# A transformer block on one core: routing weights and local values copied through DRAM instead of through TensorE

## The reference

```python
xn = layernorm(x)
# attention: 16 heads of 8 dimensions, causal; 4 heads see all earlier keys, 12 see the last 32
qkv = xn @ w_qkv + b_qkv
w = softmax(where(mask, -inf, q k^T * 8 ** -0.5))
s = (w v) @ w_out + b_out
# mixture of experts: E = 16 experts, 4 are used for a token
scores = sigmoid(xn @ gate_w.T)
cw = top-4 of the allowed groups, normalised, * 2.5, 0 elsewhere     # [tokens, 16]
act = silu(xn Wg[e]^T) * (xn Wu[e]^T)                                # 64 wide for each expert
y = sum over e of cw[:, e] * act[e] @ Wd[e]^T  + shared expert
out = x + s * silu(xn + y)
```

## Time and profile before

| | |
|---|---|
| median of 3 runs | 541.29 us (541.35, 535.84, 541.29) |
| the profiled execution's own time | 535.39 us |
| its span, first to last instruction | 533.6 us |
| TensorE's mean granted clock | 0.988 |
| busy: PE, DVE, ACT, POOL | 479.1, 347.8, 329.1, 269.0 us |
| one BODY section | about 122 us |

### The profile page before, as it was taken

The page is one execution under the profiler, slowest core; times in us unless marked ns, Lnnn a source line. Parts: engine busy times, 40 slices in busy tenths (PEclk is TensorE's granted clock), DMA queues, the critical chain, the costliest instruction groups (busy, mean ns, idle before and its releaser), DMA issues.

```text
span 533.6 us, 10570 instructions
## 1 busy us (share of the span) xinstructions
PE 479.1 (90%) x3832; PEld 286.6 (54%) x3832; DVE 347.8 (65%) x755; ACT 329.1 (62%) x654; POOL 269.0 (50%) x239
## 2 busy tenths in 40 slices
PE   1859978899999989899999988999999998989995
PEld 0647554555446755555446765545546765544442
DVE  7876439775977638776787546776788532676414
ACT  3536753767956554666957556475976566366972
POOL 3407942265737852254655872145664963016623
PEclk9979999999999999999999999999999999899998
DMA  9275374000450575000350387000170178000001
GB/s 214 79 177 100 57 99 66 1 1 2 121 77 1 164 97 78 1 1 1 116 83 1 93 153 94 2 1 1 32 159 9 40 125 133 4 2 0 1 1 39
DMA packets 144077, 32.37 MB, mean 61 GB/s; under 512 B 120966, under 2 KB 136346, under 8 KB 144026
## 3 DMA queue, kind: packets, MB, share of 16 engines
q1 hardware_dynamic: 143696, 31.41, 30.4%
q10 hardware_dynamic: 330, 0.30, 0.3%
HBM read 22.25 MB, written 9.44 MB: 59 GB/s over the span
## 4 chain that ended last, share of the span: by engine, by line
PE 56%; DVE 13%; ACT 8%; issue 7%; SPq 6%; POOL 3%; DMA 3%; DVEq 2%; POOLq 1%; ACTq 0%
PE bank L791 8%; PE bank L739 6%; PE bank L708 5%; PE bank L678 5%; PE bank L572 4%; SPq L536 4%; PE bank L574 4%; PE bank L573 4%; PE bank L755 3%; ACT stage L936 2%; DVE mxp L1176 2%; DMA kall<-planes 2%; PE bank L646 2%; PE bank L779 2%; PE bank L715 2%
## 5 line engine op out<-in xcount | busy, mean ns | idle before, releaser
L936 ACT ACTIVATE stage<-bank 128x512 f32<-128x512 f32 (+3 forms) x240 | 112.7, 539 | 59.2 <-PE bank L712 27.9
L1253 POOL TENSOR_TENSOR wrow<-wrow,gates 128x512 f32<-128x512 f32 x64 | 82.5, 1289 | 90.6 <-ACT wrow L865 90.0
L1176 DVE TENSOR_REDUCE mxp<-bank 128x1 f32<-128x512 f32 (+4 forms) x192 | 89.8, 516 | 23.7 <-PE bank L681 14.2
L1262 POOL TENSOR_TENSOR hid<-hid,wrow 128x512 f32<-128x512 f32 x64 | 82.4, 1287 | 28.4 <-DVE hid L1140 23.5
L1245 POOL TENSOR_TENSOR maxd<-mxp,k 128x512 f16<-128x512 f32 x32 | 34.7, 1083 | 95.9 <-DVE mxp L1178 51.2
L791 PE MATMUL bank<-hid,down_w 128*128 128x512 f32 x144 | 76.0, 618 | 0.0
L1140 DVE SCALAR_TENSOR_TENSOR hid<-hid,bank 128x512 f32<-128x512 f32 x72 | 48.7, 677 | 39.5 <-PE bank L574 28.6
L854 ACT ACTIVATE hid<-bank 128x512 f32<-128x512 f32 x72 | 43.7, 606 | 44.2 <-PE bank L574 44.2
L1178 DVE TENSOR_REDUCE mxp<-bank 128x8 f32<-128x512 f32 x48 | 30.9, 686 | 49.3 <-PE bank L690 49.0
L678 PE MATMUL bank<-kall,qpad 128*128 128x512 f16 (+4 forms) x192 | 52.2, 320 | 10.6 <-DVE mxp L1176 3.7
L572 PE MATMUL bank<-xh,up_hi 128*128 128x512 f32 x144 | 58.7, 408 | 2.0 <-DVE hid L1140 1.2
(11 more groups left out here) (158 smaller groups left out, 907.7 us busy)
## 6 DMA issues: line engine op xcount, KB each, us to landing
planes<-qkh SPq DMA_DIRECT2D x16, 256.0 KB, 3.2
qtmp<-planes SPq DMA_DIRECT2D x16, 256.0 KB, 3.2
kall<-planes SPq DMA_DIRECT2D x16, 256.0 KB, 3.5
qpad<-planes SPq DMA_DIRECT2D x128, 32.0 KB, 2.8
kpad<-planes SPq DMA_DIRECT2D x48, 64.0 KB, 3.3
xin<-in_L_attn_x_dram SPq DMA_DIRECT2D x4, 512.0 KB, 4.5
planes<-qkl SPq DMA_DIRECT2D x8, 256.0 KB, 3.4
xres<-in_L_attn_x_dram SPq DMA_DIRECT2D x4, 512.0 KB, 3.7
```

Of the source, the lines that this page charges most:

```text
L936: act.activation(prob[:, t % NPROB, 0:cols], ps[:, 0:cols], ACT.Exp).then_inc(freed, 1)
L1176: ins = dve.tensor_reduce(mxp[:, c, j:j + 1], ps[:, 0:cols], AX_X, ALU.max)
L1253: pool.tensor_tensor(row, row, gates[:], ALU.mult).then_inc(gated, 1)
L1262: pool.tensor_tensor(hid[:, i % NHID, :], hid[:, i % NHID, :], wrow[:, (EP * c + t) % NWT, :] if t < EP else gates[:], ALU.mult)\
```

## The change

The routing weights are halved on their way to `cwT` (the factor 0.5 was in `pairsel`), kept in plain f32, and stored by SP in DRAM as `cw_rows`. `load_weights` then loads the rows of two pairs at once into one of three slots of `wrow`: two DMAs of 64 partitions by two rows of 512, each row read 64 times. SP issues loads 0 and 1 of each batch, ACT the other six, at the even `up` steps, behind the copy to `gates`. Before it issues one, ACT waits until POOL has done the product (`hid_ready`) that last read the slot. The matmul L779, its PSUM tile and ACT's copy L865 go, and `pairsel` too.

The local values are copied by ACT to `vn` (f32), stored by SP in DRAM (`v_rows`) and loaded into the diagonal blocks of `vbd` by twelve DMAs, one for each local head, each of 32 partitions by 32 blocks by 8 values (32 B a row). Each is a step of its own (`v`) that only SP takes part in. The matmuls L639 and L640, DVE's split and its masked copies go. The first local `pv` of a batch waits for all twelve.

The three orders are new. The number of `up`, `score`, `max` and `pv` steps is as before.

```diff
-FIRST_ORDER = ("IPIIPPIPPIPTITPPTPTTIPITITIVIITPITXIXVVPXXPVVPPXXPVXIPVVXXPPXPXXVXVXX")
+FIRST_ORDER = ("PIIPPIPIPIVPVTPPTPTTTPVTTPTTPIIIIVIIXVXIXVXPXXPXVVXXVVVVVPIPPPXPXVXIPIXXX")
...
+        def load_weights(eng, n):
+
+            c, t, slot = n // (EP // 2), 2 * (n % (EP // 2)), n % NWS
+            for side in range(2):
+                row = cw_rows[2 * t + side:2 * t + side + 3:2, chunk(c)]
+                eng.dma_start(wrow[I * side:I * (side + 1), 2 * slot:2 * slot + 2, :],
+                              row.unsqueeze(0).broadcast_to([I, 2, CH])).then_inc(wrow_loaded[slot], 16)
...
+                    elif kind == "vn":
+                        c = s[1]
+                        sp.wait_ge(emptied[at.bank(s)], at.taken(s))
+                        if at.next:
+                            sp.wait_ge(v_loaded, 16 * 4 * GLOBAL * at.next)
+                        sp.dma_start(v_rows.rearrange("(t p) d -> p t d", p=P)[:, TPC * c:TPC * (c + 1), :],
+                                     vn[:, TPC * c:TPC * (c + 1), :]).then_inc(v_stored, 16)
+                    elif kind == "v":
+                        g, h = divmod(s[1], 4)
+                        if s[1] == 0:
+                            if at.section is FIRST:
+                                sp.wait_ge(v_zeroed, 1)
+                            else:
+                                sp.wait_ge(pv_done, b * SCORES_BEFORE[HG] + SCORES_BEFORE[GLOBAL])
+                            sp.wait_ge(v_stored, 16 * NCH * (at.next + 1))
+                        own = slice(HD * h, HD * (h + 1))
+                        sp.dma_start(vbd[BLK * h:BLK * (h + 1), :, g, own],
+                                     v_rows[:, BLK * g:BLK * (g + 1)][:, own].rearrange("(j k) d -> k j d", k=BLK)).then_inc(v_loaded, 16)
+                    elif kind == "cwT":
+                        c = s[1]
+                        sp.wait_ge(emptied[at.bank(s)], at.taken(s))
+                        if at.next and c == 0:
+                            sp.wait_ge(hid_ready, at.next * NCH * NUP - 1)
+                        sp.dma_start(cw_rows[:, chunk(c)], cwT[:, chunk(c)]).then_inc(cw_rows_stored, 16)
+                        if c == NCH - 1:
+                            sp.wait_ge(cw_rows_stored, 16 * NCH * (at.next + 1))
+                            for n in range(NWS - 1):
+                                load_weights(sp, n)
...
-                        ps = fill(at, s)
-                        used = ps[:, 0:TPC * GLOBAL * BLK]
-                        pe.matmul(used, repeat[:, i, :], vn_hi[:].rearrange("p t d -> p (t d)"), start=True, stop=False)
-                        done(at, s, pe.matmul(used, repeat[:, i, :], vn_lo[:].rearrange("p t d -> p (t d)"), start=False, stop=True))
...
+                        if g == 0 and n == 1:
+                            pe.wait_ge(v_loaded, 16 * 4 * GLOBAL * (b + 1))
...
-                                done(at, s + (x,), pe.matmul(ps[:], pairsel[:, t, :], cwT[:, chunk(c)], start=True, stop=True))
...
-                        if t < EP:
-                            iw = EP * c + t
-                            act.wait_ge(filled[at.bank(weight)], at.filled(weight))
-                            if iw >= NWT:
-                                act.wait_ge(hid_ready, of * NCH * NUP + (NUP * ((iw - NWT) // EP) + (iw - NWT) % EP + 1))
-                            act.activation(wrow[:, iw % NWT, :], banks[at.bank(weight)][:], ACT.Copy)\
-                                .then_inc(emptied[at.bank(weight)], 1)
+                        n = (EP * c + t) // 2 + NWS - 1
+                        if t < EP and t % 2 == 0 and n < LOADS:
+                            if n >= NWS:
+                                last = 2 * (n - NWS) + 1
+                                act.wait_ge(hid_ready, of * NCH * NUP + NUP * (last // EP) + last % EP + 1)
+                            act.wait_ge(cw_rows_stored, 16 * NCH * (of + 1))
+                            load_weights(act, n)
```

More of the change, by code:

```diff
@@ L57 @@
 NHID = 5
-NWT = 3
+NWS = 3
+LOADS = NCH * EP // 2
+LOADS_OF = [len(range(slot, LOADS, NWS)) for slot in range(NWS)]
 SPLIT_PAIR = 6
@@ L192, in value_stream @@
 def value_stream():
-    return [step for c in range(NCH) for step in [("vn", c)] + [("v", c, i) for i in range(4)]]
+    return [("vn", c) for c in range(NCH)] + [("v", i) for i in range(4 * GLOBAL)]
 def context_stream():
@@ L242, in __init__ @@
             ring = EXP if s[0] in ("up", "weights", "xT", "q", "k", "gate") or ahead else ATT
-            parts = [s] if s[0] != "up" else [s + (x,) for x in ("weight", "gate", "up") if x != "weight" or s[2] < EP]
+            parts = [s] if s[0] != "up" else [s + (x,) for x in ("gate", "up")]
             for part in parts:
@@ L408, in build @@
         hi_ready = sem("hi_ready")
-        vn_hi_ready = sem("vn_hi_ready")
+        v_zeroed = sem("v_zeroed")
+        v_stored = sem("v_stored")
+        v_loaded = sem("v_loaded")
         fold_ready = sem("fold_ready")
         sums_ready = sem("sums_ready")
-        cw_hi_ready = sem("cw_hi_ready")
+        cw_rows_stored = sem("cw_rows_stored")
+        wrow_loaded = [sem(f"wrow{slot}_loaded") for slot in range(NWS)]
         small_loaded = sem("small_loaded")
@@ L1144, in walk @@
                         continue
-                    elif kind in ("weights", "small", "vbias", "vn", "v", "cwT", "max", "outT"):
+                    elif kind in ("weights", "small", "vbias", "max", "outT"):
                         ps, freed = banks[at.bank(s)], emptied[at.bank(s)]
@@ L1248, in walk @@
                     elif kind == "up" and s[2] < EP:
-                        gate, weight = s + ("gate",), s + ("weight",)
-                        row = wrow[:, (EP * s[1] + s[2]) % NWT, :]
+                        gate = s + ("gate",)
+                        n = EP * s[1] + s[2]
+                        slot = n // 2 % NWS
+                        row = wrow[:, 2 * slot + n % 2, :]
                         pool.wait_ge(emptied[at.bank(gate)], at.taken(gate))
-                        pool.wait_ge(emptied[at.bank(weight)], at.taken(weight))
+                        pool.wait_ge(wrow_loaded[slot], 2 * 16 * (at.of(s) * LOADS_OF[slot] + n // 2 // NWS + 1))
                         pool.tensor_tensor(row, row, gates[:], ALU.mult).then_inc(gated, 1)
```

85 lines of the change are left out of this document (30 added, 55 removed).

## The result

The changed kernel takes 562.64 us (median of 4 runs, 559.8 to 564.3), the kernel before took 538.57 beside it (median of 4). The ratio is 1.044, with a 95% interval from 1.035 to 1.053: 24 us slower, where I forecast 18 to 20 us faster. The profiled execution took 564.3 us, with a span of 562.5.

A forecast was written before the change was run, and what follows sets the result against it. PE was taken as the bound everywhere, POOL close behind in boundaries. Terms 20.6 + 2 - 2 - 0 - 3 = 17.6 us off 535.4 gave 517.8, or 523.7 by the median; forecast 521 us, 8-in-10 range 505 to 534.

The forecast's parts named there:

- Steps 1 and 2: On PE, removing 64 spreading matmuls saves 15.4 us and 32 value pairs 11.2: 26.6 in all, 20.6 arriving.
- my terms for bodies and boundaries: Of PE's saving, four bodies give 9.6 us in full and three boundaries 3.0 us each, 9 us in all.
- The opening: At the kernel's start, 38 to 61 us: PE loses 4.2 us of work, 2 us gained, between -2 and 4.2.
- Step 3: On ACT, 64 copies to wrow become 48 DMA issues of 0.47 us: 2 us gained, between 0 and 6.
- Step 4: ACT's new wait for POOL's hid product at even steps: 2 us lost, 5 us at most.
- Step 5: SP's new work at batch starts: v_loaded just hidden, 0 lost; group 1's strips and pads late, 3 us lost.
- The rival of late values: Before the first local pv, dear 32-byte packets make vbd loads late and the kernel slower, up to 598 us; 5%.
- The rival of POOL and ACT: POOL and ACT replace PE as bound, boundaries give 2.1 us each: 6 us gained, 529 to 535 us; 13%.
- The new orders: Scores and maxima moved by some places in a body: 0 in the sum, 4 us either way in the range.

The follow-up runs named there:

- e7: Changed kernel with the values' stores and loads and the routing weights' loads done for batch 0 only: 526.3 us, ratio 0.978.
- e11: Kernel before, in its old orders and with weights by matmul, but values by DMA, multiplied, stored and loaded in mid-body: 538.0 us, ratio 1.002.
- e1: Kernel before in the new orders alone, routing weights and values still by matmul: 571.9 us, ratio 1.060.
- after: The changed kernel itself, with new orders and both values and weights by DMA, against the kernel before: 562.64 us, ratio 1.044.
- e5: Changed kernel, values and weights by DMA, put back in the old orders: 602.8 us, ratio 1.120.
- e8: Changed kernel in the old orders, with the value loads of groups 1 and 2 issued behind group 1's pads: 611.1 us, ratio 1.137.
- e2: Kernel before in the new orders, with routing weights by DMA and values still by matmul: 562.1 us, ratio 1.044.
- e14: Changed kernel with a quarter of the weight loads' packets in batches 1 to 3, values in full: 538.3 us, ratio 1.002.
- e9: Changed kernel with all issues, but a quarter of the packets of weight and value loads in batches 1 to 3: 531.4 us, ratio 0.989.
- e13: Changed kernel with the twelve value loads a batch issued from ScalarE's queue instead of SP's: 572.1 us, ratio 1.063.

## Why the prediction was wrong

**Steps 1 and 2, PE's part, held.** PE's busy time fell by 21.1 us; in e7, where the mean granted clock is 0.963 (0.936 in the changed kernel), by 26.0, against my 26.6. A f16 matmul still leaves its extra to the next product: L612 at 108.83, L613 at 109.24. Bodies and end gave 19.5 us, where my terms for bodies and boundaries were 18.6. But the agreement is partly luck. In e11's boundary, in the old orders, some 4.5 us less of PE's work gave 1.0 us; and from e1 to after, in the new orders, the bodies fall by 42 us where PE lost less than 27.

**The opening failed: +2 predicted, -7.2 measured.** I wrote that new orders bring routing ahead of most weight transposes, and counted that as a gain. In the new orders PE waits once for DVE's `cw`, 10.9 us, and in every experiment with the new orders, with or without DMAs, it does (8.3 to 13.3 us, e1's the longest). In the old orders (before, e5, e8, e11) it doesn't. e1, without any new DMA, opens in 72.2 us; e11, in the old orders and with the values by DMA, in 62.0. I also priced SP's round trip for the weights by issues and landings on an idle queue, and the DMA share was 0.90 from 38 to 69 us and POOL waited 16.6 us for the first `wrow`. But e2, with that round trip, opens in the same 72.2 us as e1.

**Step 3** priced a weights' issue at 0.47 us; it is 0.62. ScalarE's time was no bound either way. The error is in what this step left out: 64 copies of 0.62 us on ScalarE became 64 broadcasts of 256 KB, 1.1 us of all 16 DMA engines each. I counted the issues and the landing and no transfer, and took the landing from `kpad`, 3.3 us, where these took 5.0. e14 is the measure of what I left out: 24.3 us for three quarters of the packets of batches 1 to 3.

**Step 4 held.** ScalarE waits for POOL's `wrow` 10 times, 7.6 us in all, where it was 8 times and 5.8. The new wait ahead of its load issues, for POOL's `hid`, comes at 12 of the 24 loads, at most 1.4 us each and 12.6 in all; my forecast had about 1.3 us each, up to 20 times. What of it reaches the end is not shown.

**Step 5 is the one that failed.** I wrote that "`v_loaded` is just hidden" and took 3 us for the strips and pads of group 1. I compared SP's chain of 17.5 us with PE's 18, each by its own durations. `v_loaded` itself was hidden: PE has no wait for `vbd`. What failed is the other half, the strips and pads that stand behind the loads. The issues' durations were taken from queues with room: 0.66 us for a `vbd` load, and the median is indeed 0.65. But ten took 9.98 us, four of `kpad` 6.04, and the landing of `qpad`, `xin` and the rest came behind them. The local stages lost 41.1 us, step 3's transfers among the causes, against 3 in the sum (at most 5). The earlier trace rows had the DMA column in front of me, 0.22 in the boundary. I never asked what it is in the stretches that follow: 0.78 and 0.77 in the kernel before, and the mean of 0.32 over the body hides it.

**The rival of late values** had the right sign and the wrong mechanism. It asked for 32-byte packets that are dear. They take 9 ns; a load would have had to take 1.3 us for it to decide, and ten took 9.98 us, 1.0 each. By the Trainium skill's rule that transfers below 512 B miss line rate (*DMA: Bandwidth & Descriptors*, Specifications) I had made this the part that could fail. The trace agrees on the rate, 32 B in 9 ns (3.6 GB/s on an engine) beside 2 KB in 139 (15 GB/s). But the bytes are few: the weights' packets of 2 KB take 18 us of all engines a batch, those of 32 B 7. And what waited was not the first local `pv` but the maxima of group 1, for `qpad`. **The rival of POOL and ACT** fits the boundary of the old orders (e11) and not that of the new ones: POOL is busy 9.83 of 10 us in a window of it, and the gain arrives all the same (24.0 us from the last score to the next batch's first, where it was 27.5).

**The new orders** I put at 0 with 4 us either way. Alone they cost 33 to 35 us (e1 by its ratio and by its median, against its kernel before, 537.0), and with the DMAs they are worth 40 (e5 against after). A term of that size can't be read from where the letters moved; that the cause of e1's long bodies is a certain wait is not shown here.

What stays open: how much of the 36.4 us is SP's issuing and how much the packets' own lateness at the engines. e9 and e14 show that both shrink with the packets; e13 does not part them either, since it moved the wait along with the issues. No version here beats the kernel before with the whole computation in it; e11 equals it.

## What to carry to other kernels

Moving work from a compute engine to DMA is a move from one engine to another: price it as bytes and packets on the 16 engines over the stretch in which they fall, and read the DMA share of that stretch and of the next, not the mean over the span. An issue's duration and a landing taken where the queues are empty hold only where they stay so. An order that was worked out for one mechanism is part of it: here it gained 40 us with the one and lost more than 30 with the other.

## What the runs showed of the hardware

- A packet of 32 bytes took 9 ns of an engine's time (8225 of them, 48.2% of 16 engines in 9.5 us). That is cheap beside one of 2 KB: the 6144 of ScalarE's weight loads took 139 ns each, 15 times as long for 64 times the bytes.
- An issue lengthened where the DMA share was high: for `vbd` on SP from a median of 0.65 us to 3.1, and four on ScalarE took 8.9 us (share 0.99 from 193 to 203 us), in which ScalarE computed nothing.
- In an idle stretch of PE of 11.6 us (198.0 to 209.6) the granted clock went to 0.50 and stayed there until 213.7, 4.1 us after PE had work again, so that a late transfer cost more than its own wait.
